# Two layers of attention and FFN on one core: experts' rows gathered by scattered token numbers, and GELU and SiLU from ScalarE's tables in three more passes

## The chip, the cores and the metric

The kernel runs on one core of one Trainium2 chip. The metric is the device time of one execution in microseconds, which is lower when better. Between two kernels it is compared on the same chip.

## The reference, cut to what matters

Four batches of 512 tokens with 512 features pass two layers. Layer 0 has an attention-like block, then a dense FFN with tanh-GELU and, beside it, eight experts of which each token takes two. Layer 1 has an attention with 16 heads and an FFN with SiLU.

```python
# layer 0, FFN (hidden_states: x in pairs of tokens; E = 8, K = 2, H = 512, I = 2048, MI = 256)
dense_in = _rms(hidden_states, rn_pre1)
dense_out = _gelu_tanh(dense_in @ w_gate) * (dense_in @ w_up) @ w_down
probs = jax.nn.softmax(router_logits, axis=-1)
top_w, top_i = jax.lax.top_k(probs, K)
...
moe_in = _rms(hidden_states, rn_pre2).reshape(T, h)
g = jnp.einsum('th,ehm->tem', moe_in, we_gate)
u = jnp.einsum('th,ehm->tem', moe_in, we_up)
eo = jnp.einsum('tem,emh->teh', _gelu_tanh(g) * u, we_down)
moe_out = jnp.einsum('te,teh->th', aff, eo).reshape(b, s, h)
# layer 1, FFN: silu(x @ w_gate.T) * (x @ w_up.T) @ w_down.T, hidden size 2048
```

The kernel computes only the chosen experts: the tokens' rows are grouped by expert into blocks of 256 rows, and each block is multiplied with one expert's weights.

## The kernel before

**Passes and tiles.** TensorE's main work is a list of 174 tiles (`MAIN`). A dense pass F(f,b), layer f and batch b, has 16 tiles of 128 hidden units; the experts' pass has 23 blocks of 256 rows with two tiles each. The order is F(0,0), F(0,1), experts, F(0,2), F(0,3), F(1,0), F(1,1), F(1,2), F(1,3), so tile 16 opens F(0,1), tile 32 the experts, tile 78 F(0,2). A dense tile is 12 matmuls for the gate (PSUM bank 0), 12 for up (bank 1) and 12 for down; each product takes three matmuls, since every operand is held as a high and a low part. The downs of four tiles form a group of 48 matmuls, issued behind the first tile of the next group.

**Around a tile.** ACT reads the gate from bank 0 into `act`, DVE multiplies it by up (L1655, which gives bank 1 back), ACT writes the high part of `hid` (L1383), DVE the low part (L1661 or L1663). How the activation is made depends on `mode(s)`: "gelu" is one table pass of ACT (L1369), which gives bank 0 back. "poly", in F(0,2) and F(0,3), is Square on ACT (L1373), two DVE steps (L1643, L1644), Tanh on ACT (L1377) and a DVE step (L1649), which gives bank 0 back. "silu", in all of F(1,b), is Tanh on ACT (L1371) and L1649. Passes F(0,0), F(0,1), the experts and F(1,0) take raw weights (`raw`, two buffers) that ACT and DVE split (L1399, L1670); F(0,1) and F(1,0) also store the split weights (`w_dram`) for the later passes.

**Experts' rows.** POOL writes zeroes over the grouped rows in DRAM (`xg_dram`, L1098, 23 writes of 512 KB). Once the router's ranks and `slot` are known, it loads the normalized rows back (L1108, 8 x 512 KB) and scatters them to `xg_dram` (L1118, 32 indirect DMAs, two per 128 tokens, each row of 2 KB to its slot). SP then loads block after block into `xs` (L948, two buffers), TensorE turns it (`xgt`, L1184). The experts' outputs go to `y_dram` and are fetched by `slot` (L1160) in F(0,2) and F(1,0), where the rows' sums, norms and the queries are made ("mid" work, mostly DVE's: L1860 to L1914).

**Keys.** SP loads the keys' inputs (`kload`, L961 to L966), POOL prepares (L1057 to L1133) and scales them (L1139), ACT squares them for their norm (L1503), TensorE turns them (`kturn`, L1302), then POOL makes the queries' tables (`qtab`).

**Order.** Each engine works through its own list in order, and a wait holds all behind it. The lists come from a planner (`merge`): it places the main tiles and some 50 side streams by their dependences (`builds_on`), by costs per step (`steps`) and by sizes of DMAs (`MOVED`). A cost that is changed there moves instructions on all engines and computes nothing else.

## Time and profile before

| what | us |
|---|---|
| median of 3 runs | 1904.25 |
| lowest, highest | 1895.87, 1905.53 |
| the profiled execution | 1901.84 |
| its span, first to last instruction | 1900.1 |
| its mean granted TensorE clock | 0.949 |

| engine | busy us | share |
|---|---|---|
| PE, matmul | 1708.6 | 90% |
| DVE | 1190.2 | 63% |
| ACT | 805.2 | 42% |
| POOL | 248.8 | 13% |

PE is TensorE, DVE VectorE, ACT ScalarE, POOL GpSimd, SP the engine that issues most DMAs. The shares are means over passes of different kinds, so the passes are read one by one. Idle time of an engine is given with what released it; PEclk is the share of full clock that was granted.

### The profile page before, as it was taken

How to read it: one execution, taken by the hardware profiler on the slowest of the kernel's cores; microseconds unless marked ns; L12 is line 12 of the kernel's file. 1: busy time of each engine (PE TensorE's matmuls, PEld its weight loads, DVE VectorE, ACT ScalarE, POOL GpSimd, SP SyncE). 2: the span in 40 equal slices, each digit the busy share in tenths (PEclk: the TensorE clock that was granted, in tenths of full speed). 3: DMA queues.
4: the chain of work that ended last, by engine and by line, in shares of the span. 5: the costliest groups of instructions: out<-in, count | busy, mean ns of one | idle time of the engine just before them, and what ended most of it. 6: DMA issues, size and time to landing. Idle time of an engine off the chain costs nothing.

```text
span 1900.1 us, 27374 instructions
## 1 busy us (share of the span) xinstructions
PE 1708.6 (90%) x9396; PEld 1351.9 (71%) x9396; DVE 1190.2 (63%) x2583; ACT 805.2 (42%) x1802; POOL 248.8 (13%) x253
## 2 busy tenths in 40 slices
PE   4678899789988998779999999877899999999998
PEld 3467687668988986567667767665776678678887
DVE  5789775365656647985666766799656563553332
ACT  4456552234666643322645554442245462431110
POOL 1225324390000004110000000321100000000000
PEclk7788899899999999889999999899999999999999
DMA  3356669888889886659534415888972546236562
GB/s 107 127 189 223 231 226 354 328 326 323 272 293 321 260 323 237 204 188 319 191 95 133 139 57 178 338 318 306 301 229 79 150 129 216 82 126 203 193 217 89
DMA packets 135464, 409.52 MB, mean 216 GB/s; under 512 B 15136, under 2 KB 29856, under 8 KB 129568
## 3 DMA queue, kind: packets, MB, share of 16 engines
q1 hardware_dynamic: 125200, 372.65, 57.5%
q0 software_dynamic: 10128, 35.13, 4.9%
q8 instruction: 76, 1.25, 0.3%
q14 instruction: 60, 0.49, 0.1%
HBM read 282.95 MB, written 124.78 MB: 215 GB/s over the span
## 4 chain that ended last, share of the span: by engine, by line
PE 60%; DVE 18%; DMA 7%; issue 7%; ACT 4%; POOL 2%; SPq 1%; another core or an unknown queue 0%; POOLq 0%; ACTq 0%; DVEq 0%
PE ps L1178 16%; PE ps L1180 15%; PE ps L1179 15%; PE ps L1326 5%; DMA raw<-in_ffn_w 4%; PE ps L1335 3%; PE ps L1318 2%; DVE gu L1670 2%; POOL xg_dram L1118 2%; DVE act L1655 1%; PE ps L1184 1%; DVE wd L1670 1%; DMA gu<-w_dram 1%; ACT hid L1383 1%; DVE va L1741 1%
## 5 line engine op out<-in xcount | busy, mean ns | idle before, releaser
L1178 PE MATMUL ps<-xT,gu 128*128 128x512 f32 (+1 forms) x1392 | 541.3, 389 | 96.2 <-DVE gu L1670 29.6
L1179 PE MATMUL ps<-xT,gu 128*128 128x512 f32 (+1 forms) x1392 | 517.6, 372 | 0.0
L1180 PE MATMUL ps<-xT,gu 128*128 128x512 f32 (+1 forms) x1392 | 517.0, 371 | 0.0
L1178 PEld LDWEIGHTS ps<-xT,gu 128*128 128x128 f32 x1392 | 273.3, 196 | 156.6 <-issue 55.3
L1180 PEld LDWEIGHTS ps<-xT,gu 128*128 128x128 f32 x1392 | 272.1, 195 | 44.9
L1179 PEld LDWEIGHTS ps<-xT,gu 128*128 128x128 f32 x1392 | 273.4, 196 | 36.8
L1178 PE MATMUL ps<-wd,hid 128*128 128x512 f32 x604 | 249.2, 413 | 17.7 <-DVE acc L1690 5.3
L1180 PE MATMUL ps<-wd,hid 128*128 128x512 f32 x604 | 239.4, 396 | 0.0
L1179 PE MATMUL ps<-wd,hid 128*128 128x512 f32 x604 | 239.3, 396 | 0.0
L1383 ACT ACTIVATE hid<-act 128x512 fp32r<-128x512 f32 (+1 forms) x174 | 100.0, 575 | 265.5 <-DVE act L1655 260.7
L1670 DVE TENSOR_TENSOR gu<-raw,gu 128x512 fp32r<-128x512 f32 x188 | 135.5, 744 | 78.8 <-ACT gu L1399 72.1
L1545 ACT ACTIVATE Pr<-ps,mnb 128x128 f32<-128x128 f32 (+3 forms) x256 | 132.6, 525 | 93.1 <-DVE mnb L1922 62.3
L1655 DVE TENSOR_TENSOR act<-act,ps 128x512 f32<-128x512 f32 (+1 forms) x174 | 106.6, 613 | 96.7 <-PE ps L1180 79.5
L1178 PEld LDWEIGHTS ps<-wd,hid 128*128 128x128 f32 x604 | 116.3, 193 | 43.1 <-DVE x L1690 7.2
L1399 ACT ACTIVATE gu<-raw 128x512 fp32r<-128x512 f32 x188 | 110.4, 623 | 72.6 <-DMA raw<-in_ffn_w 35.3
L1180 PEld LDWEIGHTS ps<-wd,hid 128*128 128x128 f32 x604 | 115.7, 191 | 25.4
L1179 PEld LDWEIGHTS ps<-wd,hid 128*128 128x128 f32 x604 | 116.1, 192 | 19.6
L1649 DVE SCALAR_TENSOR_TENSOR act<-act,ps 128x512 f32<-128x512 f32 x96 | 65.8, 686 | 76.3 <-ACT act L1371 63.0
L1326 PE MATMUL ps<-ident,Pr 128*128 128x128 f32 x640 | 103.7, 285 | 3.9 <-DVE x L1950 3.0
L1371 ACT ACTIVATE act<-ps 128x512 f32<-128x512 f32 x64 | 38.2, 597 | 138.3 <-PE ps L1180 136.5
L1160 POOL DMA_INDIRECT ya<-y_dram,slot x16 | 16.1, 1007 | 608.2 <-DMA postB<-in_rn_post 319.7
L1663 DVE SCALAR_TENSOR_TENSOR hid<-act,hid 128x512 fp32r<-128x512 f32 x96 | 66.4, 692 | 43.8 <-ACT hid L1383 41.3
(273 smaller groups left out, 2420.7 us busy)
## 6 DMA issues: line engine op xcount, KB each, us to landing
gu<-w_dram SPq DMA_DIRECT2D x160, 512.0 KB
raw<-in_ffn_w SPq DMA_DIRECT2D x94, 768.0 KB
wd<-w_dram SPq DMA_DIRECT2D x80, 512.0 KB, 5.4
w_dram<-gu SPq DMA_DIRECT2D x32, 1024.0 KB
w_dram<-wd SPq DMA_DIRECT2D x32, 512.0 KB
QT<-q_dram SPq DMA_DIRECT2D x48, 256.0 KB, 5.8
xg_dram<-zt POOLq DMA_DIRECT2D x23, 512.0 KB, 5.4
x<-xg_dram SPq DMA_DIRECT2D x23, 512.0 KB, 5.9
```

What stands on the lines that cost most here:

```text
L1178: mm(out_ap, ah, bh, start=start, stop=False)
L1179: mm(out_ap, ah, bl, start=False, stop=False)
L1180: return mm(out_ap, al, bh, start=False, stop=stop)
L1326: last = turn(ps[:, 6, rows(h)], Pr[:, n % 2, h, rows(kt)], ident[:, :])
L1335: last = mm(ps[h * HD:(h + 1) * HD, 7, 0:P], Vb[:, kt, g * HD:(g + 1) * HD], PT[:, (nth("values", *a) - 1) % 3, rows(h)], start=kt == 0, s ...
L1383: func(hid[:, s % 5, 0, 0:W], act[:, s % 2, 0:W], ACT.Copy, scale=half(s)).then_inc(hid_high, 1)
L1399: func(to, raw[:, r % 2, m, :], ACT.Copy).then_inc(w_high, 1)
L1545: last = func(Pr[:, n % 2, h, 0:L], ps[:, 4 + p % 2, at:at + L], ACT.Exp, bias=mnb[:, n % 2, h:h + 1], scale=-1.0, accum_out=smb[:, n % 2, ...
L1649: stt(out=o, in0=o, scalar=1.0, in1=z, op0=ALU.add, op1=ALU.mult).then_inc(free[0], 1)
L1655: tt(out=act[:, s % 2, 0:W], in0=act[:, s % 2, 0:W], in1=ps[:, 1, 0:W], op=ALU.mult).then_inc(free[1], 1)
L1663: stt(out=hid[:, s % 5, 1, 0:W], in0=act[:, s % 2, 0:W], scalar=half(s), in1=hid[:, s % 5, 0, 0:W].bitcast(F32), op0=ALU.mult, op1=ALU.sub ...
L1670: tt(out=of[:, 1, :], in0=raw[:, r % 2, m, :], in1=of[:, 0, :].bitcast(F32), op=ALU.subtract).then_inc(w_low, 1)
```

## The change

**Rows.** The zeroed `xg_dram` and its scatter go. POOL writes zeroes once over a small table of numbers (`row_dram`, 5888 words). When the slots are known, 32 indirect DMAs scatter token numbers, 4 bytes each, to it (`place` is the slot, transposed so that the table can be loaded with 46 numbers on each partition). SP loads the table into `row_of` ("tokload"). The block's rows are then gathered by POOL, two indirect DMAs for a block, straight from `xhat_dram`. The scatter has no row reload, so the keys' load no longer depends on it.

**Activations.** "gelu" and "silu" become one mode "table"; F(0,2) now has GELU from the table, F(1,0) and F(1,3) have SiLU from the table (in F(0,3) "poly" stays, in F(1,1) and F(1,2) Tanh).

**Planner.** The keys' preparation and the queries' tables are cut into six pieces each, and some costs are changed, which moves instructions.

```diff
     def mode(s):
         kind, f, b, _ = MAIN[s]
-        if f == 1:
-            return "silu"
-        return "poly" if kind == "F" and b >= 2 else "gelu"
+        if kind == "F" and (f, b) in ((0, 3), (1, 1), (1, 2)):
+
+            return "tanh" if f else "poly"
+        return "table"
...
-            "qsum": [("POOL", 1.3)], "qt": [("PE", 0.36), ("ACT", 0.48), ("DVE", 0.6)], "inv": [("DVE", 0.4)], "values": [("PE", 0.36)], "norm": [("PE", 0.1), ("ACT", 0.3), ("DVE", 0.25)],
+            "qsum": [("POOL", 1.3)], "qt": [("PE", 0.36), ("ACT", 0.48), ("DVE", 0.6)], "inv": [("DVE", 0.4)], "values": [("PE", 0.47)], "norm": [("PE", 0.22), ("ACT", 0.3), ("DVE", 0.25)],
...
-            "scatter": lambda: [("slots", 1), ("zero", NB - 1), ("xsload", b)],
-            "xsload": lambda: [("scatter", b - 4)] if b > 3 else [("x1store", n) for n in range(B)] + [("xstore", B - 1, n) for n in range(TB)],
-            "xs": lambda: [("scatter", NT // 2 - 1 - n) for n in range(4)] if b < 2 else [("xgt", b - 2, RB - 1)],
+            "scatter": lambda: [("slots", 1), ("zero", 0)], "tokload": lambda: [("scatter", n) for n in range(NT // 2)],
+            "xs": lambda: [("tokload",)] + [("x1store", n) for n in range(B)] + [("xstore", B - 1, n) for n in range(TB)] if b < 2 else [("xgt", b - 2, RB - 1)],
...
-                elif kind == "xs":
-                    k = a[0]
-                    for h in range(4):
-                        sp.wait_ge(xg_filled[h], 64 * (NT // 8))
-                    sp.wait_ge(xg_turned, nth("xgt", k - 2, RB - 1))
-                    load(xs[:, k % 2, :, :], xg_dram[k * R:(k + 1) * R, :].rearrange("(t p) d -> p t d", p=P)).then_inc(xs_loaded[k % 2], 16)
+                elif kind == "tokload":
+                    sp.wait_ge(rows_placed, 16 * 2 * NT)
+                    load(row_of[:, :], row_dram.rearrange("(p n) o -> p (n o)", p=P).bitcast(mybir.dt.uint32)).then_inc(row_of_loaded, 16)
...
+                elif kind == "scatter":
+                    n = a[0]
+                    if n == 0:
+                        pool.wait_ge(rows_zeroed, 16)
+                        pool.wait_ge(slots_ready, 1)
+                    for t in (2 * n, 2 * n + 1):
+                        for k in range(2):
+                            nc.gpsimd.indirect_dma_start(row_dram, bass.IndirectOffsetOnAxis(ap=place[:, k, t:t + 1], axis=0), tokens[:, t:t + 1], None).then_inc(rows_placed, 16)
+                elif kind == "xs":
+                    k = a[0]
+                    if k == 0:
+                        pool.wait_ge(row_of_loaded, 16)
...
+                    pool.wait_ge(xg_turned, nth("xgt", k - 2, RB - 1))
+                    for j in range(RB):
+                        n = RB * k + j
+                        nc.gpsimd.indirect_dma_start(xs[:, k % 2, j, :], None, xhat_dram, bass.IndirectOffsetOnAxis(ap=row_of[:, n:n + 1], axis=0)).then_inc(xs_loaded[k % 2], 16)
...
-                    if mode(s) == "gelu":
-                        func(o, z, ACT.Gelu_apprx_tanh).then_inc(free[0], 1)
-                    elif mode(s) == "silu":
+                    if mode(s) == "table":
+                        func(o, z, ACT.Silu if MAIN[s][1] else ACT.Gelu_apprx_tanh).then_inc(free[0], 1)
+                    elif mode(s) == "tanh":
                         func(o, z, ACT.Tanh, scale=0.5).then_inc(tanh_ready, 1)
```

Where the instructions stand: POOL, from the end of the row work to the keys, before (`xg_dram` is the grouped rows, `kcos` the first of the keys' preparation):

```order
L1094 TENSOR_TENSOR yT<-xU,rnp 128x512 x2
L1108 DMA x<-xhat_dram 128x2x512 x4
L1118 DMA xg_dram<-x,slot 5888x512 x16
L1108 DMA x<-xhat_dram 128x2x512 x4
L1118 DMA xg_dram<-x,slot 5888x512 x16
L1057 TENSOR_TENSOR kcos<-kwB,cosB 128x128
```

POOL now, from the last step of the keys' preparation (L1138) to the queries' tables (L1151):

```order
L1138 TENSOR_TENSOR k_mul<-k_mul,k_rot 128x512 x4
L1109 DMA row_dram<-tokens,place 5888x1 x32
L1144 TENSOR_TENSOR k_mul<-k_mul,krs 128x512 x4
L1120 DMA x<-xhat_dram,row_of 128x512 x8
L1151 TENSOR_SCALAR qwB<-qwB 128x1024
```

The keys' preparation moved from behind the scatter to ahead of it; the scaling stands between scatter and gathers.

SP around the keys' load (L961 to L966, `kv_raw` to `qwB`), in the middle of F(0,1), before:

```order
L899 DMA w_dram<-gu 128x2048
L900 DMA w_dram<-wd 128x1024
L948 DMA x<-xg_dram 128x2x512 x2
L961 DMA kv_raw<-in_ctx 128x16x128
L962 DMA cosB<-in_cos 128x4x32
L963 DMA sinB<-in_sin 128x4x32
L965 DMA kwB<-in_k_w 128x128
L966 DMA qwB<-in_q_w 128x512
L965 DMA kwB<-in_k_w 128x128
L966 DMA qwB<-in_q_w 128x512
L843 DMA raw<-in_ffn_w 128x1536
```

SP around the same load now, at the end of F(0,0) (`xt_dram` are the transposed rows of the first layer):

```order
L887 DMA xt_dram<-xst 1024x1x128 x2
L847 DMA raw<-in_ffn_w 128x1536
L962 DMA kv_raw<-in_ctx 128x16x128
L963 DMA cosB<-in_cos 128x4x32
L964 DMA sinB<-in_sin 128x4x32
L966 DMA kwB<-in_k_w 128x128
L967 DMA qwB<-in_q_w 128x512
L966 DMA kwB<-in_k_w 128x128
L967 DMA qwB<-in_q_w 128x512
L847 DMA raw<-in_ffn_w 128x1536
```

It moved ahead by nine raw loads and no longer stands behind a load of grouped rows.

DVE in F(0,2), behind the rows' sums of two token tiles (`dn`, `xm`), before:

```order
L1889 SCALAR_TENSOR_TENSOR dn<-dn,rf,postB 128x512
L1891 TENSOR_TENSOR xm<-xm,dn 128x512
L1893 BN_STATS st_qnorm<-xm 128x6
L1643 TENSOR_SCALAR act<-act 128x512
L1644 TENSOR_TENSOR act<-act,ps 128x512
L1604 TENSOR_TENSOR s_zfnorm<-s_yfnorm 128x2
L1605 TENSOR_TENSOR s_zfnorm<-s_zfnorm,s_vfnorm 128x2
L1606 SCALAR_TENSOR_TENSOR s_yfnorm<-s_zfnorm,s_yfnorm 128x2
L1649 SCALAR_TENSOR_TENSOR act<-act,ps 128x512
L1655 TENSOR_TENSOR act<-act,ps 128x512
```

DVE now, at the same place:

```order
L1900 SCALAR_TENSOR_TENSOR dn<-dn,rf,postB 128x512
L1902 TENSOR_TENSOR xm<-xm,dn 128x512
L1904 BN_STATS st_qnorm<-xm 128x6
L1662 TENSOR_TENSOR act<-act,ps 128x512
L1611 TENSOR_TENSOR s_zfnorm<-s_yfnorm 128x2
L1612 TENSOR_TENSOR s_zfnorm<-s_zfnorm,s_vfnorm 128x2
L1613 SCALAR_TENSOR_TENSOR rf<-s_zfnorm,s_yfnorm 128x2
L1668 TENSOR_TENSOR hid<-act,hid 128x512
```

The three polynomial steps are gone, and the product with up (L1662, before L1655) is the first main step behind the sums.

## Rows read from the trace of the kernel before

**Rows 1.** Windows: span, busy of PE, PEld, DVE, ACT, POOL; PEclk, DMA share, GB/s.
```profile
282.90:445.30 162.40, 140.94 (x606) 113.68 (x605) 86.03 (x153) 52.30 (x117) 84.70 (x99) 0.93 0.90 339
445.30:699.00 253.70, 235.42 (x1590) 217.13 (x1590) 151.46 (x277) 153.05 (x316) 0.00 (x0) 0.97 0.85 288
699.00:880.20 181.20, 146.92 (x574) 114.00 (x573) 144.93 (x348) 56.85 (x114) 37.47 (x32) 0.90 0.70 242
...
1157.40:1341.80 184.40, 151.57 (x635) 119.81 (x634) 154.28 (x365) 71.02 (x143) 35.76 (x29) 0.93 0.79 297
...
1754.00:1900.10 146.10, 140.69 (x613) 115.69 (x611) 46.79 (x68) 19.68 (x32) 0.00 (x0) 0.99 0.49 166
```

**Rows 2.** The same view of a stretch with TensorE full, in F(1,2).
```profile
1700.00:1750.00 50.00, 50.00 (x224) 41.43 (x223) 17.65 (x26) 9.09 (x15) 0.00 (x0) 1.00 0.62 212
```

**Rows 3.** TensorE's waits in F(0,2), 699.0 to 880.2: total, times, longest us.
```profile
PE ps L1178 <- DVE act L1649: 21.3, 10, 5.5
PE ps L1178 <- DVE acc L1685: 4.7, 2, 4.5
...
PE ps L1178 <- DVE acc L1690: 3.1, 1, 3.1
```

**Rows 4.** TensorE's waits in F(1,0), 1157.4 to 1341.8.
```profile
PE ps L1178 <- DVE act L1655: 8.5, 4, 4.4
...
PE ps L1178 <- DVE act L1649: 7.1, 2, 4.6
```

**Rows 5.** TensorE's waits in F(0,1), 282.9 to 445.3.
```profile
PE ps L1178 <- DVE gu L1670: 20.0, 4, 11.7
```

**Rows 6.** Longest pause: timelines of PE and DVE (start, us), then the window.
```profile
361.83 0.76 PE L1178 MATMUL ps<-xT,gu 128*128 128x512 f32 x1 [11.68 <-DVE gu L1670]
...
359.01 0.69 DVE L1655 TENSOR_TENSOR act<-act,ps 128x512 f32<-128x512 f32 x1 [10.67 <-remote]
...
345.00:362.00 17.00, 5.32 (x24) 4.14 (x23) 3.75 (x7) 3.42 (x6) 9.08 (x10) 0.73 1.00 407
```

**Rows 7.** Timeline of POOL: first and last scatter, keys' preparation, keys' scaling.
```profile
299.76 1.07 POOL L1118 DMA_INDIRECT xg_dram<-x,slot  x1 [32.13 <-DVE tile_no L1836]
...
355.86 0.97 POOL L1118 DMA_INDIRECT xg_dram<-x,slot  x1 [0.31 <-issue]
381.41 0.46 POOL L1057 TENSOR_TENSOR kcos<-kwB,cosB 128x128 f32<-128x128 f32 x1 [24.58 <-DMA qwB<-in_q_w]
...
409.02 4.37 POOL L1139 TENSOR_TENSOR k_mul<-k_mul,krs 128x512 f32<-128x512 f32 x4
```

**Rows 8.** Timeline of SP's queue: keys' load, raw weights behind it.
```profile
368.06 0.80 SPq L961 DMA_DIRECT2D kv_raw<-in_ctx  x1
...
375.24 0.43 SPq L843 DMA_DIRECT2D raw<-in_ffn_w  x1
```

**Rows 9.** DMA issues: KB each, median us from issue to landing.
```profile
xg_dram<-x,slot POOLq DMA_INDIRECT x32, 10.4
...
ya<-y_dram,slot POOLq DMA_INDIRECT x16, 6.9
...
bk<-in_bk SPq DMA_DIRECT2D x1, 0.5 KB, 2.6
```

**Rows 10.** DVE's groups in F(0,2): count, busy, mean ns, idle before.
```profile
L1644 DVE TENSOR_TENSOR act<-act,ps 128x512 f32<-128x512 f32 x16 | 11.0, 688 | 0.6
L1649 DVE SCALAR_TENSOR_TENSOR act<-act,ps 128x512 f32<-128x512 f32 x16 | 11.0, 687 | 7.2 <-ACT act L1377 6.3 <-issue 0.7
...
L1643 DVE TENSOR_SCALAR act<-act 128x512 f32<-128x512 f32 x16 | 6.8, 422 | 15.4 <-ACT act L1373 13.8 <-issue 1.6
```

**Rows 11.** Timeline of DVE in F(0,2): first row work behind a low part, next main step.
```profile
767.35 0.24 DVE L1615 BATCH_NORM_AGGREGATE mv_qnorm<-st_qnorm 128x2 f32<-128x6 f32 x2
...
775.61 0.42 DVE L1643 TENSOR_SCALAR act<-act 128x512 f32<-128x512 f32 x1
```

**Rows 12.** ACT's table loads at L1369: ns min/median/max, first and last start.
```profile
L1369 ACT ACT_TABLE_LOAD  x5: 1283/1283/1283, 79.5 to 272.4; - x5
```

More of the change, by code:

```diff
@@ L151, in expert_ticks, with pieces_of @@
         return ticks
+    def pieces_of(kind, n):
+        return [[(kind, k)] for k in range(n)]
     def pieces(kind, b, n):
@@ L239, in steps @@
         if kind == "mix":
-            return {"gelu": [], "silu": [("DVE", 0.6)], "poly": [("ACT", 0.55), ("DVE", 0.6)]}[mode(a[0])]
+            return {"table": [], "tanh": [("DVE", 0.6)], "poly": [("ACT", 0.55), ("DVE", 0.6)]}[mode(a[0])]
         if kind == "mult":
@@ L265, in steps @@
             "rown": [("ACT", 0.71)], "pkv": [("PE", 2.73), ("ACT", 0.5), ("DVE", 0.6)], "sim": [("PE", 0.68)], "scale": [("ACT", 0.67)], "gam": [("POOL", 1.25)],
-            "bet": [("DVE", 0.75)], "aexp": [("ACT", 0.72)], "resid": [("DVE", 0.85)], "xh": [("POOL", 1.25)], "logit": [("PE", 0.85), ("DVE", 0.1)],
+            "bet": [("DVE", 0.75)], "aexp": [("ACT", 0.72)], "resid": [("DVE", 0.85)], "xh": [("POOL", 1.25)], "logit": [("PE", 0.95), ("DVE", 0.1)],
             "xt": [("POOL", 1.0), ("ACT", 0.53), ("DVE", 0.6)], "top2": [("DVE", 1.4)], "weights": [("ACT", 0.33), ("DVE", 1.2)], "ranks": [("PE", 0.36), ("DVE", 0.4)],
-            "before": [("DVE", 1.1)], "blocks": [("DVE", 1.2)], "places": [("DVE", 1.1)], "slots": [("DVE", 1.0)], "scatter": [("POOL", 5.1)], "xsload": [("POOL", 0.8)],
@@ L269, in steps @@
-            "xgt": [("PE", 0.36), ("ACT", 0.48), ("DVE", 0.6)], "kprep": [("POOL", 26.0)], "wo": [("ACT", 0.95), ("DVE", 1.15)], "ksq": [("ACT", 1.0)],
-            "kscale": [("POOL", 4.2)], "kturn": [("PE", 0.36), ("ACT", 0.5), ("DVE", 0.6)], "qtab": [("POOL", 17.0)], "fetch": [("POOL", 2.6)],
+            "before": [("DVE", 1.1)], "blocks": [("DVE", 1.2)], "places": [("DVE", 1.1)], "slots": [("DVE", 1.0)], "scatter": [("POOL", 5.1)], "xs": [("POOL", 2.55)],
+            "xgt": [("PE", 0.36), ("ACT", 0.48), ("DVE", 0.6)], "kprep": [("POOL", 4.2 if a and a[0] == 0 else 5.0 if a and a[0] > B else 4.4)], "wo": [("ACT", 0.95), ("DVE", 1.15)], "ksq": [("ACT", 1.0)],
@@ L271, in steps @@
+            "kscale": [("POOL", 4.2)], "kturn": [("PE", 0.36), ("ACT", 0.5), ("DVE", 0.6)], "qtab": [("POOL", 3.4 if a and a[0] == 0 else 2.6 if a and a[0] <= TB else 1.7)], "fetch": [("POOL", 2.6)],
             "comb": [("DVE", 1.25), ("ACT", 1.3)], "parts": [("DVE", 1.35), ("POOL", 1.3), ("ACT", 0.65)], "final": [("DVE", 2.3)], "qrow": [("ACT", 0.71), ("DVE", 1.3)],
-            "qsum": [("POOL", 1.3)], "qt": [("PE", 0.36), ("ACT", 0.48), ("DVE", 0.6)], "inv": [("DVE", 0.4)], "values": [("PE", 0.36)], "norm": [("PE", 0.1), ("ACT", 0.3), ("DVE", 0.25)],
@@ L338, in builds_on @@
[L338 to L341 removed]
+            "zero": lambda: [("gate0", 0)],
@@ L406, in leaves_bank @@
         kind, *a = item
-        return {"sim": ("scale", *a), "scores": ("exp", *a), "values": ("norm", *a[0:2]), "gate0": ("gate" if mode(a[0]) == "gelu" else "mix", a[0]) if kind == "gate0" else None,
+        return {"sim": ("scale", *a), "scores": ("exp", *a), "values": ("norm", *a[0:2]), "gate0": ("gate" if mode(a[0]) == "table" else "mix", a[0]) if kind == "gate0" else None,
                 "up0": ("mult", *a), "downs": ("down", *a[0:2])}.get(kind, item)
@@ L536, in two_layers @@
     SIDES[-B].insert(3, [("rn2",)])
-    SIDES += [[[("zero", n)] for n in range(NB)], [[("xsload", n)] for n in range(NT // 2)], routing_ticks(), key_ticks()]
+    SIDES += [[[("zero", 0)]], routing_ticks(), key_ticks()]
     for pair in range(0, B, 2):
@@ L809, in half @@
         def half(s):
-            return 1.0 if mode(s) == "gelu" else 0.5
+            return 1.0 if mode(s) == "table" else 0.5
         def unit(b, n):
@@ L1129, in _ @@
                             last = halves_swapped(k_rot[:, b * TB + t, :], kv_raw[:, b * TB + t, :], ksin[:, t, :])
-                    link(last)
-                    for b in range(B):
-                        bt = slice(b * TB, (b + 1) * TB)
-                        last = tt(out=k_mul[:, bt, :], in0=k_mul[:, bt, :], in1=k_rot[:, bt, :], op=ALU.add)
-                    link(last)
+                        link(last)
+                    else:
+                        for b in range(B):
+                            bt = slice(b * TB, (b + 1) * TB)
+                            last = tt(out=k_mul[:, bt, :], in0=k_mul[:, bt, :], in1=k_rot[:, bt, :], op=ALU.add)
+                        link(last)
                 elif kind == "kscale":
```

106 lines of the change are left out of this document (50 added, 56 removed).

## Prediction, made before the changed kernel was run

> **What bounds the kernel now.** The windows by pass [rows 1] come first, columns PE busy, DVE busy, PEclk and DMA share. In the last pass TensorE is busy for 140.7 of 146.1 us at a clock share of 0.99, and so, at 96% or more and full clock, in the three others of the five passes from 880.2 on that are not F(1,0): there it is the bound, and work taken from another engine gives nothing back. In F(0,1), F(0,2) and F(1,0) it is idle for 162.4 - 140.9 = 21.5, 181.2 - 146.9 = 34.3 and 184.4 - 151.6 = 32.8 us, with clock shares of 0.93, 0.90 and 0.93. The low level (1.2 GHz) follows the pauses, and each us at it loses half a us of matmul; by the shares that is 0.07 x 162.4 = 11.4, 0.10 x 181.2 = 18.1 and 0.07 x 184.4 = 12.9 us. So these three passes hold 33, 52 and 46 us that is not matmul at full pace. The floor agrees: with TensorE full, a 512-column matmul costs 50/224 = 0.223 to 0.225 us [rows 2], so a dense tile (36 of them) costs 8.1 us, and F(0,1) with its 16 tiles and 28 short transposes some 133 us against 162.4.
>
> Then what ends the pauses. In F(0,2) it is the DVE: 21.3 of them wait for L1649, the last step of the GELU polynomial [rows 3], while DVE is busy for 144.9 of 181.2 us. In F(1,0) five producers share them; L1649 has 7.1, the product L1655 8.5 [rows 4]. In F(0,1) 20.0 us wait for L1670, the split of fresh weights [rows 5], in four pauses. The longest, 11.7 us, shows TensorE and DVE (10.7 us) idle together; DVE's ending reads "remote", no instruction of the profile ended it, and the DMA share is 1.00 at 407 GB/s just there [rows 6]. That is while the scatter writes: its 32 instructions run from 299.8 to 356.8 [rows 7]. Behind it SP is held: it waits for the scatter's landings before the loads of blocks 0 and 1 and the keys' load behind them, at 368.1, and the raw weights queued behind them go out at 375.2 only [rows 8]; the second pause, 4.5 us, comes of that.
>
> **F(0,1): gather instead of scatter.** Removed: 23 zero writes of 512 KB, 8 reloads of 512 KB and 32 row scatters of 256 KB, 12.1 + 4.2 + 8.4 MB; the blocks' own reads stay the same 23 x 512 KB. In F(0,1) DMA share was 0.90 at 339 GB/s, and about 12 MB of its 55 MB go, so the saturated stretch and its 11.7 us pause should go, and with the scatter no longer ahead of the keys' load in SP's queue the 4.5 us too. With each goes half of the slow clock behind it: of the 11.4 us, 16.2/21.5 = 8.6. Together 24.8.
>
> New on POOL: the keys' preparation (27.6 us, from 381.4 to 409.0 [rows 7]) now stands ahead of the scatter, 32 scatters of 4-byte numbers behind it, then the keys' scaling, then the gathers. POOL generates the scatters as before: 32 of them span 57.1 us less the 14.7 between the two halves, 42.4. Timing on TensorE at full pace: tile 16's gate ends at 282.9; the slots are now ready behind tile 18's low part, 282.9 + 2.7 + 10.9 (group's downs) + 10.9 + 1.5 = 309 (before, the first scatter goes with them at 299.8 [rows 7]). The preparation starts once the keys land, about 276 to 284 by my reading of SP's order, and ends at 304 to 312. Scatters run 312 to 354; the first batch is scaled 1.1 us later (4.37/4 [rows 7]), at 355.5. TensorE passes tile 18 at 307.2, has tiles 19 to 24 (6 x 5.4) and one group's downs (10.9) to do, 350.5, and reaches the first key transpose, within the third down product behind tile 24, at 357. Then: landings of the last scatter (10.4 us as the median of the 256 KB ones [rows 9], so at most 364), the table's load 3 (2.6 and 3.5 for the smallest loads [rows 9]), two gathers 2 x 1.28 to issue, 6.9 to land as the y rows do [rows 9]: 377. TensorE wants block 0 in tile 28's up products, 24 us behind that key transpose: 381. Both covers are thin, 1.5 and 4 us; I charge 5 us for them. ACT's 16 squarings for the keys' norm and SP's wait for the xt stores before the keys' load are only moved, to tiles 16 and 17, where the group's 10.9 us of down products stand before tile 17. Sum: 24.8 - 5 = **20 us** gained; bounds 8 (the pauses return in half) and 29 (the floor).
>
> The page DMA: Bandwidth & Descriptors of the Trainium skill (Specifications) says that a write under 512 B is done as read-modify-write, which speaks against scattering words. No row here has a 4-byte scatter. If the words landed no sooner than the slowest indirect rows of the trace, 11.7 us, the cover of 4 us would shrink to 2.7, and the sum would stay.
>
> **Experts.** The block loads leave SP's queue (23 issues of 0.37 us and their waits for transposes) and become 46 indirect gathers on POOL, idle there now. A gather is asked once block k-2 is turned and needed two blocks later; a block takes 253.7/23 = 11 us, so 20 us of cover against 2.6 + 6.9 = 9.5. I take 0, with -4 to +6 because DMA share is 0.85 and the order shifts.
>
> **F(0,2): GELU from the table.** Removed from DVE per tile: L1643 0.42, L1644 0.69, L1649 0.69 [rows 10], 16 times, 28.8 us, leaving 116 of 181; the low part stays at 0.69. From ACT goes one of two passes (0.60 and 0.63). Bank 0 is given back by ACT 0.6 us behind the gate, not behind three DVE steps. The 21.3 us of waits for L1649 go, with their share of the slow clock, 21.3/34.3 x 18.1 = 11.2: 32.5. What is late next: DVE's queue still holds long runs of the rows' norms and sums between two main steps (from 767.4 to 775.6 there are 8.2 us of them [rows 11]), and the product L1655 now stands behind such a run, its bank 1 wanted 2.7 us after up ends. I charge one such rest, 4.5. Gain **28 us**; bounds 14 (two of three waits come back at L1655) and 44 (the 7.8 us of waits for L1685 and L1690, which stand in the same queue, go as well: 29.1 and 29.1/34.3 x 18.1 = 15.4).
>
> **F(1,0): SiLU from the table.** DVE loses L1649, 16 x 0.69 = 11.0 us of 154.3 [rows 1, 10]. The 7.1 us of waits go, with 7.1/32.8 x 12.9 = 2.8 of the clock; one more table load falls into it, 1.28 us on an ACT that is busy for 71 of 184 us. The whole queue being 11 us shorter where it is 84% busy, 0 to 10 more could come. I take **10 us**, bounds 4 and 20.
>
> **At nothing.** F(1,3) is TensorE's: 16 fewer L1649 are 11 us of DVE where it is busy for 46.8 of 146.1. Three further table loads (1.283 each [rows 12]) lie on ACT. The 22 issues of zeroes (0.75) leave POOL in the first pass, and the row work there is reshuffled: 0, -6 to +6. F(0,3) and F(1,1) take over a few of the rows' transposes; TensorE's work is the same, so 0 +- 3. Two small DVE steps and one more before the slots: under 1 us, counted in 309.
>
> **Sum** against the profiled execution's 1901.8 (span 1900.1 and 1.7 around it): 20 + 28 + 10 = 58, giving 1843.8. The median of the three runs is 1904.3, 2.4 above; I forecast **1845**.
>
> **Rivals.** (1) *The wait moves to L1655.* DVE's runs of row work, not the removed steps, hold TensorE: F(0,2) gives 12, F(1,0) 3, F(0,1) 20: 1868. For it: the 8.2 us run, and L1655 as the main wait in F(1,0). Against: 21.3 us name L1649. (2) *The gather chain is late.* Keys' preparation, 42 us of scatters, landings, table, gathers stand in a row with covers of 1.5 and 4 us; if word scatters or the keys' load come 20 us late, TensorE waits in tile 24 or 28 for what F(0,1) gained: 1865. (3) *All three reach their floors*: 29 + 44 + 20 = 93: 1811. (4) *Slower*: the gathers fall behind in the experts' pass. A gather that takes L from issue to landing paces two blocks, so each block waits (L + 2.6 - 22)/2; the gain is used up, and over 10 us more lost, from (58 + 10)/21 = 3.2 us a block, L = 26, with 1914 then. The longest indirect landing in the trace is 11.7. (5) *It does not do what it says*: the passes are held by dependent row work alone and F(0,1) by weights alone, so that half of the 11.7 us comes back: about 1897.
>
> **How the numbers follow.** As computed 0.54; (1) 0.20; (2) 0.11; (3) 0.08; (4) 0.03; (5) 0.04. Bounds of the sum: gains of 8 + 14 + 4 = 26 to 93, and +-6 for shifted order: the low end is 1815, the high end, where (1) and (2) lie inside and bad order is added, 1880. About 0.5% is what a measurement of this kernel tells from no change. Faster by more: 0.92; within: 0.04; slower: 0.04.
>
> **What would show it.** Right: no pause over 2 us in F(0,1) except under 5 us at a key transpose or block 0; F(0,1) near 142, F(0,2) near 153, F(1,0) near 174 us; no L1649 wait in F(0,2); experts within 254 +- 6. Wrong: a long TensorE wait for k_mul or for x<-xhat_dram in tiles 24 to 28, DVE product waits of 20 us in F(0,2), or block transposes waiting in each expert block.

## The result and the profile after

The forecast was 1845 us, with 1815 to 1880 as its range. Measured: 1896.7 us as the median of 20 executions (1889.5 to 1904.7) against 1904.6 for the kernel before; the ratio is 0.9956, 95% interval 0.9946 to 0.9967. That is 8 us faster where 59 were forecast, and outside the range. The unaltered kernel was run again on three occasions, on chips that are numbered here as the results give them: 1870.6 us on chip 10 (ratio 0.9853, 0.9829 to 0.9876), 1896.6 and 1897.0 us on chip 7 (0.9971, 0.9955 to 0.9986, and 0.9962, 0.9942 to 0.9982). The chip of the first measurement isn't known. So there are two questions: what takes 26 us in some of these measurements, and why the gain is some 30 us (1900.2 to 1870.6 by the medians on chip 10, 33.5 by the two profiled executions) and not 59 where that doesn't happen.

The windows by pass of the changed kernel, in the first profile; columns as in [rows 1]. In order: F(0,1), experts, F(0,2), F(0,3), F(1,0), F(1,1), and a stretch inside F(0,1):

```profile
276.70:448.60 171.90, 144.04 (x610) 115.23 (x609) 91.82 (x172) 52.46 (x119) 83.76 (x103) 0.90 0.71 254
448.60:702.20 253.60, 232.96 (x1584) 216.08 (x1584) 153.12 (x276) 150.93 (x317) 41.17 (x38) 0.97 0.84 289
702.20:852.30 150.10, 132.92 (x567) 105.88 (x566) 114.46 (x295) 45.21 (x96) 37.10 (x31) 0.97 0.78 279
852.30:1144.80 292.50, 274.33 (x1889) 195.64 (x1888) 176.59 (x371) 147.84 (x409) 1.30 (x1) 0.97 0.45 137
1144.80:1319.70 174.90, 152.77 (x665) 121.58 (x664) 137.32 (x320) 69.62 (x142) 33.19 (x28) 0.92 0.85 308
1319.70:1567.50 247.80, 238.15 (x1561) 174.68 (x1560) 144.44 (x327) 114.06 (x330) 5.16 (x4) 0.98 0.55 169
344.00:362.00 18.00, 4.74 (x9) 2.10 (x8) 1.21 (x2) 0.52 (x1) 14.04 (x15) 0.58 0.02 1
```

The two passes that the forecast held for unchanged, F(0,3) and F(1,1), in the kernel before:

```profile
880.30:1157.50 277.20, 271.37 (x1916) 193.35 (x1915) 175.20 (x368) 145.10 (x406) 0.00 (x0) 1.00 0.45 139
1341.90:1578.50 236.60, 232.97 (x1557) 170.89 (x1557) 136.05 (x296) 111.13 (x326) 3.87 (x3) 1.00 0.56 173
```

F(0,2) fell from 181.2 to 150.1 us and F(1,0) from 184.4 to 174.9, as forecast. F(0,1) rose from 162.4 to 171.9, F(0,3) from 277.2 to 292.5 and F(1,1) from 236.6 to 247.8.

**The stall in F(0,1).** The last window shows it: 9 matmuls in 18 us, no DMA traffic (share 0.02, 1 GB/s), and hardly anything but POOL at work. TensorE's and DVE's timelines there (start, us, then the idle time in brackets and what ended it); first the end of the third and of the fourth down product (L1187 on `wd`), then single gate matmuls, then DVE's copies of the four products (L1692):

```profile
331.10 0.39 PE L1187 MATMUL ps<-wd,hid 128*128 128x512 f32 x1
335.49 0.50 PE L1185 MATMUL ps<-wd,hid 128*128 128x512 f32 x1 [4.00 <-DVE acc L1692]
...
339.51 0.58 PE L1187 MATMUL ps<-wd,hid 128*128 128x512 f32 x1
...
353.69 0.59 PE L1187 MATMUL ps<-xT,gu 128*128 128x512 f32 x1 [2.21 <-issue]
355.80 0.59 PE L1185 MATMUL ps<-xT,gu 128*128 128x512 f32 x1 [1.51 <-issue]
```

```profile
326.92 0.69 DVE L1692 COPY acc<-ps 128x512 f32<-128x512 f32 x1 [1.23 <-PE ps L1187]
334.74 0.69 DVE L1692 COPY acc<-ps 128x512 f32<-128x512 f32 x1 [7.13 <-remote]
...
350.21 0.69 DVE L1692 COPY acc<-ps 128x512 f32<-128x512 f32 x1 [13.57 <-remote]
361.48 0.69 DVE L1692 COPY acc<-ps 128x512 f32<-128x512 f32 x1 [10.58 <-remote]
```

The third product ended at 331.5 and was copied at 350.2, 18.7 us later; the fourth ended at 340.1 and was copied at 361.5. "Remote" says that a semaphore was updated just then, but that no instruction of the profile ended just then. The trace also holds the times of the semaphores' updates: those of TensorE for the four products came 0.8, 5.9, 18.7 and 21.4 us after the products' ends, where all 19 updates of the same stretch in a run without the stall (e7 below) came within 0.01 us. So TensorE's signals are late; whether its last write was late too can't be told, since the ends of matmuls are modelled. Meanwhile TensorE gets on by one matmul in some 2 us, with "issue" as the reason, so it waited for nothing that the profile shows. All this time POOL issues its scatters at an even pace, from 316.07 (before: 299.76 [rows 7]) to 356.11, and the last late update comes 4.7 us after the end of the last one. SP has nothing to load because it waits for the weights' buffers, which DVE doesn't give back: the empty queues are a consequence.

**The wait in F(0,3).** TensorE's waits there, of which the kernel before has 5.8 us in all (277.2 - 271.4):

```profile
PE ps L1325 <- DMA QT<-q_dram: 10.3, 1, 10.3
PE ps L1185 <- DMA gu<-w_dram: 3.7, 2, 2.7
```

The first scores wait for the queries. The granted clock of the pass falls from a share of 1.00 to 0.97.

**F(0,2).** What is left there, of the 21.3 us of L1649 [rows 3]: the product, now L1662, and the sum L1697:

```profile
PE ps L1185 <- DVE act L1662: 9.8, 4, 3.8
PE ps L1185 <- DVE acc L1697: 5.1, 2, 2.8
```

### The profile page after: what moved, and what is told of

It reads as the page before. It is cut to its first block and busy times, and to the rows that moved or that the text cites. A ratio compares the mean times of both kernels' runs of the same rounds, so it can differ in the third digit from the quotient of the medians.

```text
span 1887.8 us, 27233 instructions
## 1 busy us (share of the span) xinstructions
PE 1700.5 (90%) x9396; PEld 1349.7 (71%) x9396; DVE 1145.1 (61%) x2506; ACT 797.8 (42%) x1789; POOL 269.6 (14%) x270
## 5 line engine op out<-in xcount | busy, mean ns | idle before, releaser
L1187 PE MATMUL ps<-xT,gu 128*128 128x512 f32 (+1 forms) x1392 | 514.5, 370 | 4.0 <-issue 4.0
L1187 PEld LDWEIGHTS ps<-xT,gu 128*128 128x128 f32 x1392 | 270.0, 194 | 49.0 <-issue 5.6
L1187 PE MATMUL ps<-wd,hid 128*128 128x512 f32 x604 | 239.0, 396 | 0.0
L1662 DVE TENSOR_TENSOR act<-act,ps 128x512 f32<-128x512 f32 (+1 forms) x174 | 106.8, 614 | 157.7 <-PE ps L1187 150.8
L1376 ACT ACTIVATE act<-ps 128x512 f32<-128x512 f32 (+1 forms) x126 | 64.8, 514 | 176.6 <-PE ps L1187 166.3
L1187 PEld LDWEIGHTS ps<-wd,hid 128*128 128x128 f32 x604 | 115.6, 191 | 25.3
L1668 DVE TENSOR_TENSOR hid<-act,hid 128x512 fp32r<-128x512 f32 (+1 forms) x126 | 78.0, 619 | 59.5 <-ACT hid L1390 55.6
L1325 PE MATMUL ps<-KT,QT 96*128 96x256 f32 (+2 forms) x256 | 90.2, 410 | 12.7 <-DMA QT<-q_dram 10.3
L1333 PEld LDWEIGHTS ps<-ident,Pr 128*128 128x128 f32 x640 | 68.6, 142 | 35.2 <-issue 28.5
```

Source lines behind the costliest of these rows:

```text
L1187: return mm(out_ap, al, bh, start=False, stop=stop)
L1325: mm(ps[:, 4 + p % 2, at:at + cols], QT[:, qt % 2, h, g, :], KT[:, g, 0:cols], start=True, stop=True)
L1333: last = turn(ps[:, 6, rows(h)], Pr[:, n % 2, h, rows(kt)], ident[:, :])
L1376: func(o, z, ACT.Silu if MAIN[s][1] else ACT.Gelu_apprx_tanh).then_inc(free[0], 1)
L1662: tt(out=act[:, s % 2, 0:W], in0=act[:, s % 2, 0:W], in1=ps[:, 1, 0:W], op=ALU.mult).then_inc(free[1], 1)
L1668: tt(out=hid[:, s % 5, 1, 0:W], in0=act[:, s % 2, 0:W], in1=hid[:, s % 5, 0, 0:W].bitcast(F32), op=ALU.subtract).then_inc(hid_low, 1)
```

## Experiments

Passes are in us of the profiled execution. P stands for the changed kernel with words 512 B apart (`e4_pitch512`), on which several others rest.

| run | chip | median us | ratio (95%) | F(0,1) | F(0,2) | F(0,3) | F(1,0) | F(1,1) |
|---|---|---|---|---|---|---|---|---|
| before | | 1900 to 1905 | 1 | 162.3 | 181.2 | 277.2 | 184.4 | 236.6 |
| after, first | ? | 1896.7 | 0.9956 (0.9946-0.9967) | 171.9 | 150.1 | 292.5 | 174.9 | 247.8 |
| e7 after | 10 | 1870.6 | 0.9853 (0.9829-0.9876) | 145.3 | 149.2 | 292.9 | 173.0 | 249.5 |
| e11 after | 7 | 1896.6 | 0.9971 (0.9955-0.9986) | 172.3 | 152.9 | 291.0 | 173.3 | 251.1 |
| e1 tables only | 11 | 1878.0 | 0.9885 (0.985-0.9921) | 163.2 | 164.9 | 275.9 | 173.0 | 242.4 |
| e2 rows only | 11 | 1893.7 | 0.9959 (0.9939-0.9979) | 146.1 | 179.1 | 283.4 | 182.1 | 248.8 |
| e4 = P | 11 | 1869.8 | 0.9832 (0.9798-0.9866) | 147.0 | 152.1 | 292.9 | 175.2 | 249.9 |
| e9 P, queries first | 9 | 1865.3 | 0.9802 (0.9772-0.9831) | 147.9 | 151.9 | 283.9 | 176.3 | 247.2 |
| e10 P, later scores | 9 | 1886.3 | 0.9927 (0.9907-0.9947) | 147.1 | 150.2 | 282.3 | 190.8 | 248.2 |
| e14 512 B rows, both edits | 14 | 1858.8 | 0.9775 (0.9752-0.9798) | 146.8 | 150.1 | 280.1 | 178.0 | 243.1 |

### The two halves of the change

e1 is the kernel before with the change's `mode`, its orders made by the old planner; e2 is the changed kernel with the old modes:

```diff
-        if kind == "F" and (f, b) in ((0, 3), (1, 1), (1, 2)):
-            return "tanh" if f else "poly"
-        return "table"
+        if f == 1:
+            return "tanh"
+        return "poly" if kind == "F" and b >= 2 else "table"
```

> The kernel before, with GELU and SiLU from the tables in F(0,2), F(1,0) and F(1,3) and nothing else of the change; the rows' scatter and the planner's costs stay. Theory (the tables' gain is given back by the queries): F(0,2) about 150 us for 181.2 and F(1,0) about 175 for 184.4, but the first scores come when their queries are not yet there, so F(0,3) takes about 292 for 277.2 and F(1,1) about 247 for 236.6; F(0,1) stays at 162; in all about 1889. Rival (the loss in F(0,3) and F(1,1) comes of the order and the costs changed with the rows' path): F(0,3) and F(1,1) stay within 3 us of before and the time is about 1864.

> The changed kernel with the activations of the kernel before in every pass. Theory (the scattered words stall the chip and cancel what the removed row scatter gave): F(0,1) about 172 us for 162.4 with the same stretch near 344 to 362 in which TensorE hardly works, F(0,0) about 6 us shorter, F(0,2) to F(1,1) as before; about 1907. Rival (the stall belongs to the combination or to a chance of order): F(0,1) under 150 and about 1885.

e1: its span is 25.2 us shorter than before (1874.9 for 1900.1), F(0,2) 164.9 where the theory had 150, F(0,3) 275.9: nothing given back there, so the rival was right for F(0,3), and half right for F(1,1), +5.8; its total, 1878.0, lies between the two. e2: 7.8 us shorter, F(0,1) 146.1 with no stall; F(0,3) +6.2 and F(1,1) +12.2 although no activation was changed. Its theory of the stall wasn't tested: both came on chip 11, where nothing stalls (next section). The halves add up: 25.2 + 7.8 = 33.0, and e7 is 33.5 shorter; by medians on chip 11, 24.1 + 8.5 = 32.6, and P is 32.3 below the kernel before. For single passes they don't: F(0,2) gives 16.3 and 2.1 us in the halves and 31 in the whole, F(0,3) -1.3 and +6.2 in the halves and +15.3 in the whole.

### Where the stall comes, and where not

e3 scatters 512 B rows (the number in the first word), e4 words at a pitch of 512 B, e5 moves the table in DRAM, e6 changes the last pass alone:

```diff
-   indirect_dma_start(row_dram, ..., tokens[:, t:t + 1], None)      # e3
+   indirect_dma_start(row_dram, ..., tokens[:, t:t + 128], None)
-   row_dram ... y_dram                                              # e5
+   y_dram ... row_dram
-        if kind == "F" and (f, b) in ((0, 3), (1, 1), (1, 2)):      # e6
+        if kind == "F" and (f, b) in ((0, 3), (1, 1), (1, 2), (1, 3)):
```

> The changed kernel with rows of 512 B scattered in place of words of 4 B: each carries the token number in its first word and the following numbers behind it, and only the first words are loaded back. Theory (a write of 4 B is what stalls): the stretch at 344 to 362 goes, F(0,1) falls from 172 to about 150 and the time to about 1875; the load of the 5888 single words may cost up to 5 of it. Rivals (it is the POOL engine's 32 indirect DMAs whatever they write, or something else in that stretch): F(0,1) stays near 172 and the time near 1897.

> The changed kernel with the same 4 B words scattered 512 B apart, so over 3 MB in place of 23.5 KB. If the size of a write stalls, F(0,1) stays near 172 us and the time near 1897. If it is their closeness (writes into the same few hundred bytes wait for each other), F(0,1) falls to about 150 and the time to about 1875. If neither this nor the 512 B rows change the stretch, the writes are not its cause.

> The changed kernel, every instruction in its place, with the table of the rows (23.5 KB) declared behind the experts' outputs, so that it lies 12 MB further on in DRAM. The words are scattered as close together as in the changed kernel. If the stall near 344 to 362 depends on where the table lies, it goes: F(0,1) about 147 us and the whole about 1871. If the close words stall whatever they lie beside, or if timing decides, F(0,1) stays near 172 and the whole near 1897.

> The changed kernel with SiLU through Tanh in F(1,3) alone, the last pass; all up to tile 158 is the same work in the same order, but the programs of ACT and DVE have another length. The last pass should take 146.0 for 144.4 us. If the stall in F(0,1) is a property of the close words and of the work around them, F(0,1) stays near 172 and the whole near 1898. If it hangs on how the program lies in memory, F(0,1) may fall to 147 and the whole to about 1873.

All four had F(0,1) at 146 to 147 and 1867.8 to 1872.5 us (ratios 0.9831 to 0.9846, e3 and e4 on chip 11, e5 and e6 on chip 9). Each looked like a cure, and none was one, as the control that should have come first shows, the kernel unaltered:

> The changed kernel once more, unaltered, on the chip of this call. If the stall of F(0,1) belongs to this program (the table's place and the program's own layout), it comes again: F(0,1) near 172 us, the same stretch near 344 to 362, and about 1896. If it belonged to the occasion and not to the program, F(0,1) takes 147 and the whole about 1869, as in the kernels whose table or last pass alone was moved.

> The changed kernel unaltered, once more, on the chip of this call. Of this program two things are known: 20 executions at a median of 1896.7 us, the profiled one with a stall at 344 to 362, and 4 executions at 1870.6 us on another chip without it. If the stall belongs to the occasion (the chip, or where its memory is given), this call shows either, and F(0,1) takes 172 or 146 us with all other passes alike; if the first result was a rarity, it is 146 us and about 1870 again.

e7, on chip 10: F(0,1) 145.3, no stall. e11, on chip 7: 172.3, with the trickle of "issue" pauses from 348 to 363, and all 10 executions lie between 1893.9 and 1900.5. A second pair on chip 7:

> The changed kernel unaltered, as the control on the chip of this call: F(0,1) takes 172 us and the whole 1896 where the stall comes, 146 and 1870 where it doesn't.

> The changed kernel with 512 B rows scattered in place of the words, and nothing else. If the size of the write makes the stall, F(0,1) takes 147 us and the whole 1872 also where the control stalls. If 32 indirect DMAs back to back make it whatever they write, it stalls with the control, at 1896. If the control doesn't stall, both take 1870 and the pair tells nothing new.

Control 1897.0, 512 B rows 1898.1: both stall. The window 343 to 362 of e16 (columns as in [rows 1]) and two rows of its TensorE:

```profile
343.00:362.00 19.00, 5.74 (x11) 2.68 (x10) 0.69 (x1) 0.00 (x0) 15.01 (x17) 0.57 0.15 49
```

```profile
352.99 0.59 PE L1189 MATMUL ps<-xT,gu 128*128 128x512 f32 x1 [1.53 <-issue]
355.07 0.59 PE L1187 MATMUL ps<-xT,gu 128*128 128x512 f32 x1 [1.50 <-issue]
```

So on chip 7 neither the size of the write (e16) nor its distance (e12 below, at a pitch of 512 B, F(0,1) 170.5) decides. What remains is the run of 32 indirect DMAs, or what chip 7 does differently.

The late updates are a mark that any trace can be searched for. Idle time of DVE or ACT that ends "remote" and is longer than 1 us stands in six of the 20 traces: in those from chip 7 (e11, e12, e15, e16), in the changed kernel's first profile, and in that of the kernel before. In F(0,1) of the changed kernels it grows step by step: a product that ends with 8 to 12 scatters out is signalled 0.3 to 1.8 us late, the next one 4.7 to 8.3, and the worst 20 to 27; the last late update comes 4 to 5 us after the last scatter. In F(0,2) and F(1,0) updates are late once more, by up to 2.7 us, beside runs of indirect gathers of the experts' outputs; in F(0,2) that costs nothing (the changed kernel waits 4.9 us for L1662 from 720 to 775 with it, and e7 as long at the same place without).

So the first measurement bears the mark of chip 7, and the 11.7 us pause of [rows 6] in the kernel before is the same thing in small. There the gate's last matmul ended at 347.4 and the up product's at 350.2; ACT read the first at 351.9, DVE the second at 359.0, 8.8 us late:

```profile
349.77 0.39 PE L1180 MATMUL ps<-xT,gu 128*128 128x512 f32 x1
```

```profile
351.92 0.60 ACT L1369 ACTIVATE act<-ps 128x512 f32<-128x512 f32 x1 [4.31 <-remote]
```

The full queues alone aren't the cause: e1, on chip 11, has the same scatter of rows and the same load on the queues. The window 340 to 360 of before, then of e1 (columns as in [rows 1]), and e1's two longest waits of TensorE in F(0,1):

```profile
340.00:360.00 20.00, 10.15 (x45) 8.07 (x43) 4.65 (x7) 4.29 (x8) 12.96 (x13) 0.82 1.02 415
340.00:360.00 20.00, 17.14 (x71) 13.79 (x70) 7.81 (x12) 6.80 (x12) 15.10 (x16) 0.93 1.02 416
```

```profile
PE ps L1179 <- DVE gu L1671: 10.3, 4, 3.9
PE ps L1185 <- DMA x<-xg_dram: 8.2, 1, 8.2
```

Without the pause TensorE comes to block 0 earlier and waits 8.2 us for its rows (0.2 in the kernel before), so F(0,1) is as long in e1, 163.2. That fits the medians of the kernel before, 1902.5 and 1903.6 on chip 7 and 1900.2 to 1902.1 on the others. e1's order differs a little (its scatter starts 4.2 us later), and the kernel before itself was profiled only once.

Two kernels were to tell what in the run of DMAs matters; they came on chip 0, which doesn't stall. e17 waits for the landings of each eight:

```diff
+                    pool.wait_ge(rows_placed, 16 * 4 * (n - n % 2))
                     for t in (2 * n, 2 * n + 1):
```

> The changed kernel, whose POOL waits for the landings of each eight scatters before it issues the next eight; the run of 42 us becomes four of 10 us with some 2 to 4 us between. If the run without a pause makes the stall (it begins 12 to 14 scatters in), F(0,1) takes about 150 us also where the kernel beside it stalls: 147 and up to 5 for a gather chain that comes 10 us later. If pauses of this size don't help, it takes 170. Where the control doesn't stall: 147 to 152 and 1870 to 1876.

> The changed kernel with five added stretches of 32 DMAs on POOL in F(1,1) to F(1,3), into scratch: behind tile 134 scatters of 512 B rows back to back; behind 142 the same with a wait for the landings of each eight; behind 150 gathers of words back to back; behind 156 direct DMAs of 64 KB; behind 162 the scatters again. Control is the kernel's own scatter: F(0,1) 172 us where it stalls. If any unbroken run of indirect DMAs stalls such a chip, the first, third and fifth stretch cost 15 to 25 us each there and the second and fourth nothing. If it takes the full queues of F(0,1) beside them, none does. Without the stall in the control: all five nothing.

e18: 1871.8 in its single execution, all five stretches harmless. e17: 1883.1, and not 1870 to 1876. The three pauses of POOL are 5.4 + 4.8 + 4.7 = 15 us longer than a step without one, and TensorE then waits at the first key transpose:

```profile
PE ps L1310 <- POOL k_mul L1145: 10.5, 1, 10.5
```

That measures the cover of the chain, 15 - 10.5 = 4.5 us, and makes this cure a poor one: 11 us of F(0,1) for a stall that isn't there. Whether it helps on chip 7 stays open.

### Words one behind the other

e13 adds five stretches to POOL where it is idle, in F(1,1) to F(1,3):

```diff
+            probe(0, 130, word_dram, 1, 32)
+            probe(1, 140, row_dram_512, P, 32)
+            probe(2, 146, word_dram, 1, 12, spaced=True)
+            probe(3, 154, row_dram, 1, 32, gather=True)
+            probe(4, 160, word_dram, 1, 32)
```

> The changed kernel with five added stretches of indirect DMAs on POOL, which is idle there; they write or read scratch that nothing else uses. Behind tile 130: 32 scatters of words, one behind the other; behind 140: 32 scatters of 512 B rows; behind 146: 12 scatters of words, each behind the next gate or up of TensorE; behind 154: 32 gathers of words; behind 160: 32 scatters of words once more. The kernel's own scatter in F(0,1) is the control: only if it stalls (F(0,1) 172 us) do the others tell anything. Theory A (words written back to back stall, whatever else runs): stretches 1 and 5 show the same trickle of matmuls, 15 to 20 us lost each, the other three nothing. Theory B (any indirect DMAs back to back): 1, 2, 4 and 5 do. Theory C (only where the other DMA queues are full, as in F(0,1)): none of the five does. Where F(0,1) takes 147 us, all five should show nothing.

The control doesn't stall (chip 14, F(0,1) 146.3), yet the two stretches of words do harm, which none of the theories had: 1928.8 us in the single execution, F(1,1) 280.1 where P takes 249.9, and F(1,3) 171.4 for 146.3. The windows of the five, in order; columns as in [rows 1]:

```profile
1350.00:1392.00 42.00, 15.60 (x68) 12.40 (x66) 6.12 (x10) 4.37 (x9) 25.26 (x26) 0.69 1.05 117
1566.00:1608.00 42.00, 41.39 (x206) 32.95 (x203) 16.48 (x28) 11.40 (x26) 31.64 (x32) 1.00 0.71 244
1657.00:1720.00 63.00, 63.00 (x373) 48.24 (x366) 31.03 (x66) 21.04 (x42) 11.61 (x12) 1.00 0.59 135
1726.00:1768.00 42.00, 42.00 (x187) 34.80 (x186) 13.51 (x20) 6.83 (x10) 31.59 (x32) 1.00 0.57 198
1781.00:1823.00 42.00, 31.74 (x141) 25.95 (x139) 8.96 (x13) 5.41 (x9) 31.61 (x32) 0.92 0.92 110
```

This is another thing than the stall: here the queues are full (share 1.05) and move 117 GB/s only. TensorE waits for loads, 26.2 us for the queries in the first stretch; the weights' loads of 512 KB beside it took 42.5 us to land (last number):

```profile
PE ps L1347 <- DMA QT<-q_dram: 26.2, 1, 26.2
```

```profile
wd<-w_dram SPq DMA_DIRECT2D x4, 512.0 KB, 42.5
```

In the fifth it waits 23.0 us for weights. 512 B rows at the same slots, word gathers, and 12 words that are spaced in time cost TensorE at most 0.6 us in their windows. The kernel's own 32 word scatters do no such harm. They differ from the probes' in the index: `place` puts neighbouring slots 46 words (184 B) apart, the probes' `slot` puts them side by side. That this makes the difference is an inference; the source and the pass differ too.

### The queries' wait

SP issues the loads of the output projection (2 MB) and of the rows (1 MB) ahead of the first queries, in the kernel before as well. What is new is when: the queries' loads go out 5.4 us into F(0,3) before, at 20.1 us now. SP's queue, before and then now:

```profile
885.66 2.93 SPq L853 DMA_DIRECT2D QT<-q_dram  x6
```

```profile
872.37 4.33 SPq L857 DMA_DIRECT2D QT<-q_dram  x6
```

e9 turns the order of the loads round on P (here and in `rows`); e10 puts the first scores later instead:

```diff
-            "woload": lambda: [("ktload", b)],
+            "woload": lambda: [("ktload", b), ("qload", b, 0), ("qload", b, 1)],
```

> The kernel with words 512 B apart, with the queries' loads (0.75 MB) ahead of the loads of the output projection (2 MB) and of the rows (1 MB) in SP's queue, at the start of both attentions. Theory (the first scores wait for queries that lie in the queues behind 3 MB): the queries land 5 to 8 us sooner, the pause of 10.4 us before the first scores goes or falls under 4, F(0,3) takes about 282 for 292.9 us and F(1,1) about 245 for 249.9; about 1856 for 1870. Rival (it is the slower start of the clock and the row work itself, not the loads' order): F(0,3) stays above 290 and the time at 1870.

> The kernel with words 512 B apart, with the first scores of both attentions one to two tiles later (tile 98 for 97 and 134 for 132) and the loads in their old order. Theory (TensorE meets the scores before their queries have landed): the tile placed ahead of them fills the pause, F(0,3) takes about 282 for 292.9 us; F(1,1), whose pauses are short, gains at most 5; about 1858. Rival (the pause is only moved, or what is pushed back crowds the end of the attention): F(0,3) stays within 3 us of 292.9, the time within 4 of 1870.

e9: the pause falls from 10.4 to 2.3 us and F(0,3) from 292.9 to 283.9. TensorE's wait in F(0,3) in P, then in e9:

```profile
PE ps L1327 <- DMA QT<-q_dram: 10.4, 1, 10.4
```

```profile
PE ps L1327 <- DMA QT<-q_dram: 2.3, 1, 2.3
```

Time from issue to landing of the queries (last number), first in the changed kernel's first profile, then in e9:

```profile
QT<-q_dram SPq DMA_DIRECT2D x6, 256.0 KB, 17.7
```

```profile
QT<-q_dram SPq DMA_DIRECT2D x6, 256.0 KB, 12.1
```

The total gained only 4.5 of the 14 us expected (on another chip than P), F(1,1) only 2.7; the experts' pass was 5.5 us longer in this profile (257.7 for 252.2), with nothing changed there. A single profile doesn't tell that much of this pass: in the four of the unaltered changed kernel it takes 253.2 to 260.1 us. e10: F(0,3) 282.3, but with 1764 matmuls in it where e9 has 1889, a new wait for weights of 15.4 us in it, F(1,0) 190.8 for 175.2 and F(1,2) 7.5 longer. What was pushed back crowds the passes behind, as the rival said, though not by its numbers: the time is 16 us worse.

e8 is P with the planner's old costs for values, norms, projection and logits; e12 is e9 and e8 together:

> The kernel with words 512 B apart, with the planner's costs for values, norms, projection and logits as in the kernel before; it computes the same in a slightly other order. Theory (these costs are innocent, the queries lie late because the rows' path reshuffled the planner's order in F(0,2)): the last queries stand at tile 94 as before the edit, F(0,3) stays within 4 us of 292.9 and the time near 1870. Rival (the costs shape the attention's start): F(0,3) and F(1,1) fall by 10 us each, to about 1850.

> Words 512 B apart, the queries' loads ahead of the output projection's and the rows', and the planner's old costs for values, norms, projection and logits. The first gave 9 us in F(0,3) by the queries' loads, the costs 6 us. Theory (both shorten the same wait before the first scores): F(0,3) about 281 us, the time about 1863. If they are independent, F(0,3) falls to 277 and the time to 1859. The pause before the first scores stays under 3 us in both.

e8 (chip 10): 1870.7, F(0,3) 286.5 with the pause unchanged (10.7 us), F(1,1) 250.2. The costs aren't what makes the wait. They are worth 6.4 us of F(0,3), but the total stays that of P (1869.8): F(1,0) is 2.3 us longer and the experts' pass 5.1. e12 came on chip 7 and stalled: 1885.8, F(0,1) 170.5, but F(0,3) 278.6. The same two edits on the kernel with 512 B rows:

> Rows of 512 B scattered for the words, the queries' loads ahead of the output projection's and the rows', and the planner's old costs. If a write under 512 B is what stalls, F(0,1) takes about 147 us even where the changed kernel stalls, F(0,3) about 279 and the whole about 1860. If the size doesn't matter, F(0,1) takes 170 wherever the other kernel of this call does, and the whole 1885.

It gives 1858.8 us, ratio 0.9775, the fastest kernel measured here, on chip 14. As e16 shows, it has to be expected to stall on chip 7 as well.

## Why the prediction was wrong

Two steps failed: the one on F(0,1), which put the long pause down to full queues and had no term for the stall, and the one that took F(0,3) and F(1,1) at nothing. Each is worth some 27 us in the first measurement, the second on every chip.

**F(0,1), -20.** The size is right on a chip without the stall, 162.4 to 145.3, so -17; the reason given for most of it isn't, so part of that is luck. The 11.7 us pause was put down to the saturated queues that go with the row scatter. [Rows 6] showed DVE's idle time ending "remote" while POOL scattered, and e1 has the same full queues (416 GB/s) and no such pause: 8.8 us of it are late updates, and what the scatter costs on a chip without them is the 8.2 us wait for block 0. In e7 both are gone, and so is the 4.5 us pause [rows 5]. Its longest pause is 7.0 us, against the sign that none would be over 2: the product L1662 stands behind the keys' norm steps and the numbering of the rows in DVE's list, at 307.3 where up had ended at 301.1 at the latest. None is for the keys or for block 0. The slots came at 316 to 317 where 309 was worked out, but the charge of 5 us for thin covers wasn't needed; e17 puts the first cover at 4.5 us, where 1.5 had been worked out. Where the stall comes, the pass is 27 us longer, since 32 scatters in one run stand where two runs of 16 stood. That the length of the run does it isn't tested. Neither this step nor a rival had it. The nearest was rival (5), 1897: the right number, and an old pause that comes back, but for dependent row work and weights, not for late updates; that is luck too.

**The skill's rule.** The page DMA: Bandwidth & Descriptors of the Trainium skill (Specifications) has writes under 512 B as read-modify-write, and the prediction let it cost a little landing time. Here words land sooner than the 10.4 us of the old rows [rows 9]: e17's POOL, on its ninth scatter (timeline: start, us, and in brackets the idle time), waits 5.75 us for the landings of the first eight.

```profile
332.56 0.96 POOL L1110 DMA_INDIRECT row_dram<-tokens,place  x1 [5.75 <-DMA row_dram<-tokens,place]
```

Whether the rule is behind e13, where words harm everybody else's DMAs, isn't shown: the kernel's own words, 184 B apart, and those of P, 512 B apart, are as small and do no such harm.

**F(0,2), -28, and F(1,0), -10.** Right: -31.1 and -9.5 (e7: -32.0 and -11.4). What is left is what was named, products and sums behind the rows' work. The division wasn't: with the tables alone (e1) F(0,2) gives only 16, with the rows' path alone (e2) 2, and the rest needs both: it comes with the tables in the new order, in which the queries' steps stand up to three tiles later (the last query is turned at tile 94; 93 before, 91 in e1) and DVE has 114.5 us of work in the pass for 118.5.

**"At nothing".** This step failed on every chip: F(0,3) +15.3 and F(1,1) +11.2 (e7: +15.7, +12.9), where "TensorE's work is the same, so 0 +- 3" stood. The work was the same, the start of the attention was not. Before, the last query is stored 5 us ahead of F(0,3) (issued at 874.9, the pass begins at 880.3); in e1 13 us ahead; now 8 us into it (860.6, 852.3). A stretch that reads 1.00 at 98% busy has no slack against a late input, and the forecast asked for each shortened pass what it waits for, but not what the next pass expects of it. In F(0,3) that is shown: the tables alone take nothing (e1, -1.3), the new order takes 6.2 (e2), both together 15.3; the queries' loads sent ahead give back 9.0 (e9), the old costs 6.4 (e8), both 14.3 (e12 against P). In F(1,1) the cause stays open. The last query is stored later there too (35.4 us into the pass for 15.2), but no wait is over 2.3 us; TensorE's idle time in it rises from 3.6 to 9.7 us and its busy time from 233.0 to 238.2. e2 has the loss without the tables (+12.2), and e9 gives back 2.7.

**Experts 0, F(1,3) 0.** Right, as far as single profiles tell: 253.6 in both kernels, 253.2 to 260.1 in the others of the changed one; F(1,3) with Tanh (e6) and with the table (e7) took 144.4 both. Rival (4) had no part. F(0,0) gave 6.4 us, just over its bound of 6.

**The sum** on a chip without the stall: -17.0 - 32.0 - 11.4 in the three passes, F(0,0) -6.4, against +28.6 in F(0,3) and F(1,1), +3.6 in the experts', +2.0 ahead of tile 0 and -0.8 in the last two: -33.4, where the spans say 1866.6 - 1900.1 = -33.5. In the first measurement F(0,1) is 26.6 us longer than in e7, and that is the stall; the medians, 1896.7 and 1870.6, are 26.1 apart.
